# Heads 4 and 5 of samples 2 to 5 turned by DMA instead of by the matrix engine, and the next x loaded from another queue

## The reference

```python
q, k, v = x @ Wq.T, x @ Wk.T, x @ Wv.T          # 32 query heads, 8 key heads, head size 128
q, k = rope(rmsnorm(q, q_norm_w)), rope(rmsnorm(k, k_norm_w))
kc, vc = k_cache[block_table], v_cache[block_table]     # 16 pages x 32 keys per sample
k_all, v_all = concatenate([kc, k]), concatenate([vc, v])     # 512 + 128 keys
scores = where(valid, q @ k_all.T * D ** -0.5, -1e30)
probs = softmax(scores)                          # per head 128 queries x 640 keys
out = (probs @ v_all) @ Wo.T
```

## Time and profile before

| what | value |
|---|---|
| median of 3 runs | 1295.25 us (1294.81 to 1295.65) |
| profiled execution | 1296.83 us |
| its span in the trace | 1295.2 us |
| PE busy | 1276.0 us, 99% of the span |
| PEld, DVE, ACT, POOL busy | 84%, 72%, 61%, 59% |
| granted TensorE clock | 1.0 of full speed |
| DMA | 179.59 MB, mean 139 GB/s |

### The profile page before, as it was taken

One profiled execution on the slowest core, in us unless ns is written; L12 is line 12 of the kernel. 1 busy time (PEld: TensorE's weight loads), 2 busy tenths in 40 slices (PEclk: granted clock), 3 DMA queues, 4 the chain that ended last, 5 costly groups with the idle time before them and its releaser, 6 DMA issues.

```text
span 1295.2 us, 26107 instructions
## 1 busy us (share of the span) xinstructions
PE 1276.0 (99%) x6713; PEld 1092.1 (84%) x6713; DVE 935.1 (72%) x2658; ACT 785.1 (61%) x1834; POOL 765.5 (59%) x792
## 2 busy tenths in 40 slices
PE   9999999998999999999999999999999999999998
PEld 7888877887888888888888888888888888888886
DVE  6532357778777777877777788687777877777774
ACT  5731333646666668686666686765656767665664
POOL 2110011338766668687666686966667869666663
PEclk9999999999999999999999999999999999999999
DMA  8321224276655557757555577565556775555543
GB/s 280 119 82 45 77 71 140 57 268 191 130 126 124 131 129 212 179 123 150 130 129 128 137 201 186 123 133 137 131 133 157 186 186 136 127 124 124 124 98 82
DMA packets 314897, 179.59 MB, mean 139 GB/s; under 512 B 260418, under 2 KB 279234, under 8 KB 314562
## 3 DMA queue, kind: packets, MB, share of 16 engines
q1 hardware_dynamic: 295840, 125.83, 40.6%
q0 software_dynamic: 12032, 35.40, 10.1%
q10 hardware_dynamic: 6946, 17.44, 4.3%
HBM read 119.71 MB, written 16.91 MB: 105 GB/s over the span
## 4 chain that ended last, share of the span: by engine, by line
PE 80%; DVE 5%; issue 4%; SPq 4%; ACT 3%; DMA 2%; POOL 1%; ACTq 0%; POOLq 0%; DVEq 0%
PE bank L1624 16%; PE tail L1662 14%; PE wide L1692 13%; PE tail L1729 11%; PE wide L464 4%; PE wide L1656 4%; PE wide L544 3%; PE bank L1645 3%; PE tail L464 3%; PE bank L464 2%; PE wide L599 2%; SPq L1527 2%; SPq L1513 1%; PE bank L544 1%; PE bank L599 1%
## 5 line engine op out<-in xcount | busy, mean ns | idle before, releaser
L1662 PE MATMUL tail<-prT,vt 128*128 128x512 f32 (+1 forms) x975 | 257.4, 403 | 2.1 <-ACT prT L1865 1.9
L1662 PEld LDWEIGHTS tail<-prT,vt 128*128 128x128 f32 x975 | 171.9, 188 | 41.2 <-DVE prT L2089 10.1
L1343 POOL TENSOR_TENSOR tick<-tick 128x1 f32<-128x1 f32 x254 | 56.2, 221 | 212.3 <-PE tail L1662 70.7
L1729 PE MATMUL tail<-woT,oT 128*128 128x512 f32 x768 | 179.5, 389 | 0.9 <-DVE oT L2141 0.9
L1729 PEld LDWEIGHTS tail<-woT,oT 128*128 128x128 f32 x768 | 144.0, 188 | 31.2 <-DVE oT L2141 1.3
L1692 PE MATMUL wide<-kT,qT 128*128 128x320 f32 x512 | 158.6, 310 | 1.8 <-DVE mx L2117 1.5
L1692 PE MATMUL wide<-kT_low,qT 128*128 128x320 f32 x512 | 158.2, 309 | 0.0
L1692 PE MATMUL wide<-kT,qT_low 128*128 128x320 f32 x512 | 158.0, 309 | 0.0
L1401 POOL TENSOR_TENSOR parts<-raw,parts 128x1280 f16<-128x1280 f32 x55 | 145.6, 2647 | 8.0
L1884 ACT ACTIVATE raw<-raw,nm,q_scale 128x640 f32<-128x640 f32 x124 | 114.6, 924 | 47.0 <-DVE nm L2120 45.3
L1884 ACT ACTIVATE pr<-pr,nm,q_scale 128x640 f32<-128x640 f32 x128 | 118.1, 923 | 35.9 <-DVE nm L2120 35.1
(11 more groups left out here) (289 smaller groups left out, 2850.0 us busy)
## 6 DMA issues: line engine op xcount, KB each, us to landing
w_ring<-pair_weights SPq DMA_DIRECT2D x80, 256.0 KB, 4.1
k_raw<-k_pages SPq DMA_DIRECT2D x512, 32.0 KB, 1.7
v_raw<-v_pages SPq DMA_DIRECT2D x512, 32.0 KB, 2.9
spread<-one_over_denominators ACTq DMA_DIRECT2D x32, 512.0 KB, 4.9
xTb<-x_transposed POOLq DMA_DIRECT2D x31, 512.0 KB, 4.1
rope<-rope_tables SPq DMA_DIRECT2D x31, 256.0 KB, 2.7
out<-y POOLq DMA_DIRECT2D x31, 256.0 KB, 5.8
w_raw<-w_gate_up SPq DMA_DIRECT2D x10, 512.0 KB
```

The source lines that it names most:

```text
L1343: nc.gpsimd.tensor_tensor(tick[:, 2:3], tick[:, 1:2], tick[:, 1:2], ALU.add).then_inc(s_carry, 1)
L1662: last = nc.tensor.matmul(tail[g][:, first * S:end * S], vt[v_part][:, j, g * D:(g + 1) * D], prT[p_part][:, first:end, j, :], start=(j == ...
L1729: last = nc.tensor.matmul(place[:, :], oT[:, g, o_part, (h % REP) * S:(h % REP + 1) * S], woT[w_part][:, h, :], start=(h == o_part == w_pa ...
```

## The change

1. In samples 2 to 5 of every pair (`THIRDS`; 16 of the 32 units) heads 4 and 5 go the way of heads 0 to 3. POOL makes a third pair of float16 parts behind the second (`halve_third`, into `parts[0]` again, once its first transposes have landed). SP issues two more DMA transposes (`turn_third`) into `turned_third`, which lies on the place of heads 4 and 5. In the next turn ACT (`high_turned_third`) and POOL (`low_turned_third`) widen them. PE turns 10 blocks of heads 6 and 7 only, and ACT's and DVE's instructions on them have half the size.
2. In those turns PE sums all of group 0 first, its keys' transposes between, and the second group in the order: high parts of all blocks, low parts of all blocks.
3. The next x is loaded by ACT's queue, behind the squares (in third turns behind the cast of the second turned pair); POOL's `load_x` and the wait ahead of it go.
4. `spread` moves to the place of `parts[1]`; in third turns it is loaded after the cast of the new keys. `add_share` stands behind the keys in third turns.
5. SP: the loop over pairs is written out; the page tensors are laid out by pair, so that an address is page times a constant; the rope table comes ahead of the keys; the last 2 keys (5 outside third turns) come between or behind the transposes, and 14 of 16 value loads behind the third's transposes.
6. The second root of the four late turns moves behind `low_new`; PE waits for it at the score of head 1 and no more ahead of the second `probs_wide`.
7. Samples 2 and 6 are written out ahead of and behind a loop of three.

```diff
+    THIRDS = range(2, 6)
+
+    def has_third(b):
+
+        return b in THIRDS if isinstance(b, int) else True
+
+    def thirds(pair, b):
+
+        done = min(max(b - THIRDS[0], 0), len(THIRDS)) if isinstance(b, int) else b - THIRDS[0]
+        return done + pair * len(THIRDS)
+
...
+        def halve_third(u, before, n):
+
+            pool.wait_ge(s_exp, u * HP + 3 * HALF)
+            for i in range(2):
+                pool.wait_ge(s_turned[0][i], (u + before) * 16 + 16)
+            carry(n)
+            nc.gpsimd.tensor_copy(parts[0][:, 0], pr_third[:, :, :]).then_inc(s_half, 1)
+            pool.wait_ge(s_half, u * 2 + before + 3)
+            nc.gpsimd.tensor_tensor(parts[0][:, 1], pr_third[:, :, :], parts[0][:, 0], ALU.subtract).then_inc(s_rest[0], HALF)
+
+        def low_turned_third(u, before, n):
+
+            pool.wait_ge(s_turned[0][1], (u + before) * 16 + 32)
+            pool.wait_ge(s_pv, u * G + 1 + FIRST)
+            carry(n)
+            nc.gpsimd.tensor_copy(prT[1][:, 0:HALF].rearrange("p h j q -> p (h j) q"), turned_third[1]).then_inc(s_tl, 1)
...
-            if then_x is not None:
-                pool.wait_ge(s_q1, u + 1)
-                carry(n)
-                if first_turn:
-                    pool.wait_ge(s_xs[0], 16 * BLK)
-                load_x(then_x)
-                n = n + 1
...
+            if has_third(b - 1):
+                low_turned_third(u - 1, thirds(pair, b - 1), n)
+                add_share(u - 2, share, n + 1)
+                n = n + 2
...
+                halve(u, before, n + 2, 1, False, then_x is not None and extra != "next")
+                if has_third(b):
+                    halve_third(u, before, n + 3)
+                    n = n + 1
...
+        def turn_third(pair, b):
+
+            u, before = unit(pair, b), thirds(pair, b)
+            sp.wait_ge(s_rest[0], (u + before) * HALF + 2 * HALF)
+            for i in range(2):
+                sp.sem_inc(s_seen, 1)
+                sp.dma_start_transpose(turned_third[i], parts[0][:, i].rearrange("p h n -> p (h n)")).then_inc(s_turned[0][i], 16)
...
+            if has_third(b - 1):
+                load_rope(pair, b)
+                load_keys(pair, b, pages, 0, NPP - 2)
+                turn_part(pair, b - 1, 0, 0)
+                load_keys(pair, b, pages, NPP - 2)
+                turn_part(pair, b - 1, 0, 1)
+                turn_part(pair, b - 1, 1, 0)
+                turn_part(pair, b - 1, 1, 1)
+                load_values(pair, b, pages, 0, VALUES_FIRST)
+                turn_third(pair, b - 1)
+                load_values(pair, b, pages, VALUES_FIRST)
...
+                    if h and second_queries_late(pair, b, front, back):
+                        pe.wait_ge(s_second_root, second_queries_late(pair, b, front, back) * ROOT_STEPS)
...
-                if front:
-                    pe.wait_ge(s_tl, u * 2 + 2)
+                if third:
+                    pe.wait_ge(s_rope, n * G + 2 + FIRST)
+                    transposes(0, [ra[:, REP + i, :] for i in range(G)])
+                    probs_wide(1, 0)
+                    pe.wait_ge(s_tl, u * 2 + before_back + 2)
+                    sums(0, range(JT), (0,), 1).then_inc(s_pv, 1)
+                    probs_wide(1, 1)
...
-                if second_queries_late(pair, b, front, back):
-                    pe.wait_ge(s_second_root, second_queries_late(pair, b, front, back) * ROOT_STEPS)
                 probs_wide(1, 1)
...
+            if third:
+                pe.wait_ge(s_yadd, u + FIRST)
+                pe.wait_ge(s_th[0], u + before_back + 2)
+                for w in range(2):
+                    pe.wait_ge(s_phi, u * 3 + w + 1)
+                    sums(1, (2 * w, 2 * w + 1), (0, 1), 0)
+                pe.wait_ge(s_phi, u * 3 + 3)
+                sums(1, (JT - 1,), (0, 1), 0)
+                for w in range(2):
+                    pe.wait_ge(t_free[w], u + 1 + FIRST)
+                pe.wait_ge(s_tl, u * 2 + before_back + 3)
+                sums(1, range(JT - 1), (0,), 1)
+                begin(0)
+                sums(1, (JT - 1,), (0,), 1).then_inc(s_pv, 1)
...
+                if ahead and not third:
+                    load_x((b + 1) % B if isinstance(b, int) else b + 1)
...
+                if third and ahead:
+                    load_x(b + 1)
...
-            if back:
+            if back and not third:
                 spread_shares()
...
+            if third:
+                spread_shares()
+                high_turned_third()
             if back:
                 high_probs(0)
+            if third:
+                high_probs(1)
...
-                if late:
-                    inverse_root(slice(REP + G, NH), then_second)
...
+            if third:
+                low_probs(1)
...
-                low_probs(1)
+                if not third:
+                    low_probs(1)
                 low_new()
+                if late:
+                    dve.wait_ge(t_free[1], u + 1 + FIRST)
+                    inverse_root(slice(REP + G, NH), then_second)
```

More of the change, by code:

```diff
@@ L1303, in turns @@
                 turn(pair, 1, before(pair * B + 1), True, True, True, "out", True, True)
-            with eng.Fori(0, B - 3) as last:
-                turn(pair, last + 2, before(last + (pair * B + 2)), True, True, True, None, True, True)
+            turn(pair, 2, before(pair * B + 2), True, True, True, None, True, True)
+            with eng.Fori(0, len(THIRDS) - 1) as last:
+                turn(pair, last + 3, before(last + (pair * B + 3)), True, True, True, None, True, True)
+            turn(pair, 6, before(pair * B + 6), True, True, True, None, True, True)
             more = pair + 1 < NPAIR
@@ L1441, in turn @@
                 clear_bias()
-            share_room(u, share is not None)
+            if not has_third(b - 1):
+                share_room(u, share is not None)
             if extra == "out" and not first_turn:
-                low_weights(own, 4 * KT - 1, 4 * KT + 2)
+                low_weights(own, 4 * KT - 1, 4 * KT + 1)
             if first_turn:
@@ L1501, in sync, with pages_of @@
     def sync(sp):
-        def pages_of(site, b):
-            held = [sp.alloc_register(f"page{site}_{j}") for j in range(NPP)]
+        def pages_of(site, pair, b):
+            held = [sp.alloc_register(f"page{site}_{pair}_{j}") for j in range(NPP)]
             sp.load(held, table[0:1, bass.ds(b, 1), :].rearrange("p b j -> p (b j)"))
@@ L1562, in sync @@
         KEYS_FIRST = 11
+        VALUES_FIRST = 2
         def run():
-            with sp.Fori(0, NPAIR - 1) as pair:
-                with sp.Fori(0, B - 3) as b:
-                    load_unit(2, pair, b + 2)
-                pages = pages_of(6, B - 1)
+            for pair in range(NPAIR - 1):
+                load_unit(7, pair, 2)
+                with sp.Fori(0, len(THIRDS)) as b:
+                    load_unit(2, pair, b + 3)
+                pages = pages_of(6, pair, B - 1)
                 load_keys(pair, B - 1, pages)
@@ L1608, in begin @@
                 pe.wait_ge(c_free[i], full[i].value() + FIRST)
+            before_back, third = thirds(pair, b - 1), back and has_third(b - 1)
             first_turn = isinstance(b, int) and b == 0
@@ L1648, in probs_of @@
             def probs_of(g, j):
-                return [pr[i][:, j * P:(j + 1) * P] for i in range(REP)]
+                return [pr[i][:, j * P:(j + 1) * P] for i in range(HALF if third else 0, REP)]
             def probs_wide(g, w):
@@ L1774, in turn @@
                     rest.fourth_quarter()
-                pe.wait_ge(s_rope, n * G + 2 + FIRST)
-                transposes(0, [ra[:, REP + i, :] for i in range(G)])
-            if back and front:
+                if not third:
+                    pe.wait_ge(s_rope, n * G + 2 + FIRST)
+                    transposes(0, [ra[:, REP + i, :] for i in range(G)])
+            if back and front and not third:
                 sums(0, (2, 3), (0,), 1, low_heads)
-                if second_queries_late(pair, b, front, back):
-                    pe.wait_ge(s_second_root, second_queries_late(pair, b, front, back) * ROOT_STEPS)
                 probs_wide(1, 1)
@@ L1785, in turn @@
             if back and front:
-                sums(0, (JT - 1,), (0,), 1, low_heads).then_inc(s_pv, 1)
+                if not third:
+                    sums(0, (JT - 1,), (0,), 1, low_heads).then_inc(s_pv, 1)
                 transposes(0, probs_of(1, JT - 1))
-            if back:
+            if third:
[12 more added lines that the diff above has]
+                sums(1, (JT - 1,), (0,), 1).then_inc(s_pv, 1)
+            elif back:
                 pe.wait_ge(s_yadd, u + FIRST)
@@ L1828, in turn @@
             full0 = Count(c_full[0], before[0])
+            before_front, before_back, third = thirds(pair, b), thirds(pair, b - 1), back and has_third(b - 1)
+            first_head = HALF if third else 0
+            heads_there = REP - first_head
             def arrive():
```

(12 more changed lines are left out.)

212 lines of the change are left out of this document (120 added, 92 removed).

## The result

The kernel before took 1296.03 us (median of 20 runs), the changed one 1298.20 (20 runs). The ratio is 1.0019, with an interval of 1.0012 to 1.0025: no gain, and 0.2% lost. Forecast was 1271.2, with a range of 1266 to 1282.

The account below looks back on a forecast made before the run. PE's own instructions were taken as the bound (busy 1276.0 of 1295.2 us). Gains of 17.4 + 2.7 + 4.1 + 1.0 less 1.2 for hand-overs made 24.0 us, so 1271.2 us, range 1266 to 1282.

Parts of the forecast that it names:

- SP's circle with POOL: SP and POOL wait for each other in third turns: 30.1 us against a turn of 30.0; cost zero, bounds 0 and 1.1.
- the covers: Slack by which POOL's casts of turned low parts precede their need: 1.2 us for ACT, 4.1 for PE, absorbing some tenths.
- Only four times in a pair: The SP and POOL circle runs in just four turns of each pair, which was to limit its lateness.
- Rival A: The circle of SP and POOL becomes the bound: 13 of the 24.0 us gain go, about 1284 us; chance 0.11.
- Transposes taken from PE: Ten blocks fewer for PE in each of 16 turns, at 0.109 us each: 17.4 us gained.
- low-part wait: PE's second group no longer waits for DVE's low parts in third turns: 0.17 us a turn, 2.7 us gained.
- hand-overs: Allowance for unseen hand-overs between engines: 0.08 us a third turn, 1.2 us taken off.
- Late second root: PE's 5.7 us wait for `q_scale` goes, less 0.4 us new waiting in each of four turns: 4.1 us gained.
- Single wait of 1.9: One PE wait for ACT's cast of a turned pair, where 16 key loads delayed SP's transposes; half counted, 1.0 us.
- Rival B: ACT's hand-over to PE at `high_probs(0)`, cover 0.3 us, fails: 0.5 us each third turn, about 1279 us; chance 0.13.
- Rival C: `spread` lands late, delaying `mask_max(0)`: slower than before, 1308 us if landing takes 9.3 us; chance 0.03.
- Rival D: Transposes taken from PE are worth their mean of 273 ns: 43.7 us instead of 17.4, 1245 us; chance 0.01.

Follow-up runs that it names:

- s3_longer_seven: s3_longer with 7 instead of 2 value loads ahead of the third pair's transfers on SP; 1275.51 us, ratio 0.9843.
- s2_before: The kernel before, each DMA transpose replaced by two plain copies of 64 partitions (turning left out); 1293.56 us, ratio 0.9985.
- s3_longer: The changed kernel with the stand-in, the low parts of the first and third pairs copied in three pieces instead of two; 1303.27 us, ratio 1.0048.
- the three doses: SP's hand-out of turned parts per round: 7.4 us (changed kernel with the stand-in, 1278 us), 8.8 (true transposes, 1298), 9.7 (s3_longer, 1303).
- s4_root_back: s3_seven with the late second root put back to its old place, ahead of the first queries' low part; 1274.18 us, ratio 0.9842.
- the stand-in: Each DMA transpose replaced by two plain copies of the same bytes, same queue and waits, turning left out; on the changed kernel 1278.05 us, ratio 0.9863.
- s4_four_values_mask: s2_four_values with mask_keys moved ahead of the late second root; 1274.87 us, ratio 0.9844.
- s3_seven: The changed kernel with the stand-in and 7 value loads ahead of the third pair's transfers; 1276.04 us, ratio 0.9842.
- s2_four_values: The changed kernel with the stand-in, a sample's cached values loaded by 4 transfers from fixed places instead of 16 by page number; 1285.37 us, ratio 0.9920.

## Why the prediction was wrong

**The step that failed** is the cost of SP's circle with POOL, "Cost: zero, bounds 0 and 1.1 us a turn". The circle was seen and laid out, and its place in the kernel was right. It took back 21.3 us in after, 1.3 us for each of the 16 third turns, above even the upper bound. Three things in it were wrong.

- Its length. I had 30.1 us. In after, from 402.37 on: two transposes with gaps 3.2, 14 values 7.0, branch and tables 2.4, 14 keys 7.2 with 0.3 behind, a transpose 1.5, two keys 1.3, landed and seen 3.8, POOL's third 4.2, together 30.9. Each term is within some tenths of mine, but I took one value for each, for the landing the median, and the other rounds have slower ones: 8.40 us for 14 values and 3.0 for branch and tables in the first, 4.8 us for a landing in the third (456.03 to 460.87). Against a turn of 29.87 us there was no room at all, and such terms make a mean of 31.9.
- What lateness does. I counted on the covers (1.2 us to ACT, 4.1 to PE) to take up "some tenths". They did so once: the lateness is the sum over the rounds, 3.0 + 1.0 + 1.9 = 5.9 us in this pair. The covers let two turns through unharmed, and then the rest reached PE: the excess of the turns in this pair is 6.3 us.
- Where it stops. "Only four times in a pair" was to limit it. But what is late is still late in the turns of samples 7 and 0, which are then 2.2 and 1.0 us longer than before in the first pair: 8.9 of the 21.3 us fall there, in turns to which I had given no cost. Rival A, of the same mechanism, had 13 us and a chance of 0.11; both were too low.

**The other terms.**

- Transposes taken from PE, 17.4, low-part wait 2.7, hand-overs -1.2: 18.9 expected, 16 x (31.09 - 29.87) = 19.5 measured. Right (all 16 third turns have this length in s3_longer_seven), and the pace of 109 ns for one transpose, not the mean of 273, was the one to use. The wait of the weight loads for low parts is 5.2 us, 16 times, in s3_longer_seven, against 10.1 us, 32 times before: gone from the third turns.
- Late second root, 4.1: wrong, it is 0. The wait for `q_scale` did fall, from 5.7 to 2.7 us. But DVE does the same work up to `mask_max(0)`, as I had written myself, and PE can be only two scores ahead of it. So the time that PE won was waited for at the next scores, and not 0.4 us a turn of it. The weight loads of the scores show it, in before and in after (total us, times, longest):

```profile
PEld wide L1692 <- DVE mx L2117: 1.7, 3, 0.7
PEld wide L1767 <- DVE mx L2240: 4.7, 11, 0.7
```

- Single wait of 1.9, of which I took 1.0: in the trace it is gone whole, 2.2 us. In s2_before that turn has only 1.1 us too much, so the size of this wait is not firm.
- Rival B: PE waits once for ACT's `prT` of the halves in after, 0.6 us in a turn whose parts came late; as a cost of its own it is out. Rival C: `spread` lands after 4.2 us (median), and in the third turns after 5 us at most; the longest landing, 10.2 us, is in a turn of sample 0. Rival D: out, since the turns became 1.22 us shorter for ten transposes.

That the circle is enough to take the gain back, and that without it the gain stands, follows from s3_longer and s3_longer_seven. For after itself it rests on the same pattern of turns and rounds, the same waits of PE and the order of the three doses; no kernel with the true transposes was changed at this one place. With the circle and the late root out of the way (s4_root_back) the stand-in gains 1293.56 - 1274.18 = 19.4 us (18.5 by the two ratios); my sum of 24.0 without its 4.1 for the root is 19.9. So the terms of PE were sound, and the circle, costed at zero, took them back. The direction was missed too: faster was forecast with 0.95, and the kernel came out the same within 0.2%. Open is why the first 14 values of a pair took 8.40 us (7.7 to 8.6 in the four pairs), and what a kernel with the true transposes and seven values first would take.

## What to carry to other kernels

When two engines wait for each other around a loop, work out the length of that circle from its terms at their upper values, not their medians: where it is as long as the turn there is no room. Covers between the engines are spent once, not in each turn. An engine that is idle inside such a circle while it has work that could be handed out (here five page loads) is the place to change: one constant was worth 28 us where the circle was too long, and 2 us at most where it was nearly short enough. And a wait that goes from an engine is worth nothing where the next one on it, for the same other engine, ends at the same time.

## What the runs showed of the hardware

- **A DMA transpose and its hand-out.** A transpose of 128 x 1280 16-bit values holds SP for 1.3 to 1.6 us in most cases and lands 3.6 us (median in after) after its start. Two plain copies of 64 x 1280 hold it for 1.1 to 1.3 us together, and each lands 2.6 us (median) after its start. In the rounds of after the 16 DMA engines were busy for 0.70 of the time, in s3_longer for 0.56 to 0.59, with the same pattern of turns. So it is SP's time to hand out that was short here, not theirs.
- **DVE waits for POOL.** The mask takes 0.48 to 0.51 us alone and 3.15 to 3.18 us in the four cases where it began within 0.05 us behind the start of POOL's 2.92 us subtraction. It ended each time some 0.3 us behind it. Partial overlaps cost less: in after six masks took 0.8 to 1.6 us, and each ended 0.28 us behind a cast or subtraction of POOL. The Trainium skill ("SBUF — State Buffer", section "SBUF: two separate sides") says that DVE and GpSimd share a pair of ports under an exclusive lock, for DVE instructions in a two-port mode or with two SBUF inputs, and that the later one blocks until the other has ended. The trace agrees, with 3.15 us for 0.50; in which of these modes the mask ran, no run shows. DVE's `prT` subtraction, with one input in PSUM, ran beside a POOL subtraction at 527.95 for 1.23 us (rows of s4_four_values_mask), its length without one, so it is not every DVE instruction that waits. The swap of two steps on DVE gave back 10.5 us.
- **The clock.** The long turn of sample 0 in s3_seven costs 5.2 us, of which the mask's wait is 2.7. The wait reaches PE through `normalise(0)` and `mask_max(0)` on DVE:

```profile
1030.51 0.41 PE L1774 MATMUL wide<-kT,qT 128*128 128x320 f32 x1 [2.77 <-DVE mx L2247]
```

Busy time by stretch in s3_seven (length, busy time of PE, PEld, DVE, ACT and POOL, granted clock, DMA share, GB/s):

```profile
1020.00:1026.00 6.00, 5.34 (x28) 4.14 (x26) 5.41 (x21) 1.89 (x3) 3.34 (x5) 1.00 0.83 276
1026.00:1030.00 4.00, 1.74 (x9) 1.26 (x9) 3.96 (x4) 0.26 (x1) 2.69 (x1) 1.00 0.48 128
1030.00:1034.00 4.00, 3.49 (x16) 3.26 (x17) 3.79 (x13) 2.89 (x7) 0.49 (x2) 0.74 0.11 25
1034.00:1040.00 6.00, 6.00 (x31) 5.33 (x31) 4.19 (x15) 3.91 (x9) 5.71 (x5) 0.89 0.42 101
```

PE stood idle for 2.3 of 4 us, in the wait of 2.77, and then the granted clock was 0.74 and 0.89: part of that time at the lower level, 1.2 GHz. (In s2_four_values it is 0.58 from 538 to 542 us, behind the mask of 533.95.) The chain of waits of s3_seven has the same six score matmuls at both clocks:

```profile
1032.58 1.60 PE wide L1774 x6
...
1037.04 0.87 PE wide L1774 x6
```

So behind this wait PE paid a second time, up to 0.73 us for six matmuls. In before the turn of sample 0 in the first pair has this stretch, with 1.04 us idle and no loss of clock:

```profile
530.00:534.00 4.00, 2.96 (x19) 2.23 (x17) 3.62 (x18) 1.87 (x3) 2.88 (x6) 1.00 0.87 267
```
